# A head group's load in two parts, the second behind the next step's shift rows

## The reference

```python
x = x + _layernorm(attn(_layernorm(x)))
x = x + _layernorm(ffn(_layernorm(x)))
```

## Time and profile before

| | |
|---|---|
| median of three runs | 993.25 us |
| the profiled execution's own time | 992.39 us |
| its span, first to last instruction | 990.4 us |
| mean granted clock of PE | 0.999 |
| busy share of the span | PE 98%, DVE 72%, POOL 48%, ACT 39% |
| the hardware DMA queue | 144.49 MB, 47.4% of 16 engines' span |
| load of a group: queries, keys | 768 KB in 5.7 us, 192 KB in 6.1 us (medians from issue to landing) |

### The profile page before, as it was taken

The page is one execution under the profiler, slowest core; times in us unless marked ns, Lnnn a source line. Parts: engine busy times, 40 slices in busy tenths (PEclk is TensorE's granted clock), DMA queues, the critical chain, the costliest instruction groups (busy, mean ns, idle before and its releaser), DMA issues.

```text
span 990.4 us, 17190 instructions
## 1 busy us (share of the span) xinstructions
PE 973.8 (98%) x6315; PEld 801.0 (81%) x6315; DVE 716.3 (72%) x1968; ACT 382.4 (39%) x660; POOL 474.2 (48%) x478
## 2 busy tenths in 40 slices
PE   6999999999999999999999999999999999999997
PEld 6888898898886666666666679999999999999996
DVE  7778595775569999999999676666666666666655
ACT  6211120211138777787777662222222222222221
POOL 1455563644449999999998711111111111111110
PEclk9999999999999999999999999999999999999999
DMA  9764755467358777655555472332332332222201
GB/s 351 265 221 159 266 193 195 166 199 243 131 180 218 200 213 187 180 164 139 153 147 153 123 238 58 88 86 85 86 86 86 85 86 86 83 73 82 61 22 43
DMA packets 85411, 145.58 MB, mean 147 GB/s; under 512 B 7352, under 2 KB 46928, under 8 KB 82256
## 3 DMA queue, kind: packets, MB, share of 16 engines
q1 hardware_dynamic: 85328, 144.49, 47.4%
HBM read 93.07 MB, written 50.87 MB: 145 GB/s over the span
## 4 chain that ended last, share of the span: by engine, by line
PE 87%; DVE 7%; DMA 2%; issue 1%; POOL 1%; ACT 1%; POOLq 0%; SPq 0%; DVEq 0%
PE bank L1490 19%; PE bank L1492 19%; PE bank L1491 19%; PE bank L1595 8%; PE bank L1573 8%; PE bank L1611 7%; PE bank L1632 2%; PE bank L1638 1%; PE bank L1776 1%; DVE wq_l L1105 1%; DVE ln_st L1067 1%; DVE xt_l L1190 1%; DVE turn L1118 1%; DVE xt_raw L1182 1%; PE bank L1581 1%
## 5 line engine op out<-in xcount | busy, mean ns | idle before, releaser
L1141 DVE CUSTOM_DVE_ANT_0 bank<-bank,row_mask 128x384 f32<-128x384 f32 (+3 forms) x512 | 234.4, 518 | 35.9 <-PE bank L1573 35.7
L724 POOL TENSOR_TENSOR ln_rs<-ln_ve,minus_half 128x1 f32<-128x1 f32 x51 | 52.6, 1032 | 332.0 <-DVE ln_mm L1076 332.0
L940 ACT ACTIVATE prob<-bank 128x512 f32<-128x512 f32 x320 | 173.2, 599 | 24.5 <-PE bank L1595 15.7
L1492 PE MATMUL bank<-wf_l,xt_h 128*128 128x384 f32 (+3 forms) x384 | 130.1, 339 | 0.0
L1490 PE MATMUL bank<-wf_h,xt_h 128*128 128x384 f32 (+3 forms) x384 | 129.8, 338 | 0.2 <-DVE xt_l L1282 0.2
L1491 PE MATMUL bank<-wf_h,xt_l 128*128 128x384 f32 (+3 forms) x384 | 129.6, 338 | 0.0
L1490 PE MATMUL bank<-xt_h,wq_h 128*128 128x512 f32 x304 | 119.1, 392 | 0.9 <-DVE xt_l L1190 0.9
L1491 PE MATMUL bank<-xt_h,wq_l 128*128 128x512 f32 x304 | 118.5, 390 | 0.0
L1492 PE MATMUL bank<-xt_l,wq_h 128*128 128x512 f32 x304 | 118.4, 390 | 0.0
L1573 PE MATMUL bank<-k_t,q_t 96*128 96x384 f32 (+3 forms) x512 | 117.6, 327 | 0.0
L796 POOL TENSOR_TENSOR key_sum<-key_sum,prob 128x512 f32<-128x512 f32 x92 | 116.6, 1294 | 0.0
(11 more groups left out here) (131 smaller groups left out, 1931.8 us busy)
## 6 DMA issues: line engine op xcount, KB each, us to landing
q_t<-q_scratch SPq DMA_DIRECT2D x32, 768.0 KB, 5.7
q_scratch<-turn_h SPq DMA_DIRECT2D x32, 512.0 KB, 3.9
q_scratch<-turn SPq DMA_DIRECT2D x16, 512.0 KB, 4.7
att_scratch<-att SPq DMA_DIRECT2D x32, 256.0 KB, 3.0
at_raw<-att_scratch SPq DMA_DIRECT2D x16, 512.0 KB, 4.2
x<-x SPq DMA_DIRECT2D x16, 512.0 KB, 4.2
out<-z SPq DMA_DIRECT2D x15, 512.0 KB, 2.9
den_i<-inv_scratch SPq DMA_DIRECT2D x56, 128.0 KB, 5.0
```

What stands on the lines that cost most here:

```text
L724: nc.gpsimd.tensor_tensor(ln_rs[j][:], ln_ve[j][:], minus_half[:], ALU.pow).then_inc(count, 1)
L940: nc.scalar.activation(prob[n % 2][:, i, :, :].rearrange("p h q -> p (h q)"), score_bank(n, i)[:], ACT.Exp, scale=INV_SQRT_HD).then_inc(pr ...
L1141: last = nc.vector.tensor_tensor_reduce(out=row, in0=row, in1=row_mask[:, SEQ - w:SEQ], scale=1.0, scalar=LOWEST, op0=ALU.add, op1=ALU.max ...
L1492: return mm(dst, a_h, w_l, start=False, stop=stop, skip_group_check=True)
```

## The change

`load_group` gets an argument `parts`. Part 0 is the first half of the queries' columns (two heads), part 1 the other half and the keys. In SP's loop the call at the end of step n loads part 0 of group n + 4 only; part 1 of that group is issued in the next step, right behind that step's `load_shift`. A load has now three DMAs, so R0 waits for 48 counts per use of the slot instead of 32. The calls before the loop load both parts at once, as before.

```diff
-            def load_group(n):
+            def load_group(n, parts=(0, 1)):
...
-                sp.dma_start(q_dst[0:KROWS, :], q[:, cols]).then_inc(qk_loaded[s], 16)
-                sp.dma_start(k_dst[0:KROWS, :], k).then_inc(qk_loaded[s], 16)
+                half = REP * SEQ // 2
+                if 0 in parts:
+                    sp.dma_start(q_dst[0:KROWS, 0:half], q[:, cols][:, 0:half]).then_inc(qk_loaded[s], 16)
+                if 1 in parts:
+                    sp.dma_start(q_dst[0:KROWS, half:2 * half], q[:, cols][:, half:2 * half]).then_inc(qk_loaded[s], 16)
+                    sp.dma_start(k_dst[0:KROWS, :], k).then_inc(qk_loaded[s], 16)
...
             for n in range(NG):
                 if 0 < n < NG - 1:
                     load_shift(n + 1)
+                if n > 0 and n + SLOTS - 1 < NG:
+                    load_group(n + SLOTS - 1, (1,))
                 if 1 <= n < WO_LOADS:
                     load_out(n)
...
                 if n + SLOTS < NG:
-                    load_group(n + SLOTS)
+                    load_group(n + SLOTS, (0,))
...
                 if i == 0:
-                    pe.wait_ge(qk_loaded[s], 32 * (n // SLOTS + 1))
+                    pe.wait_ge(qk_loaded[s], 48 * (n // SLOTS + 1))
```

## The result

The changed kernel takes 1077.66 us (median of four runs, 1073.33 to 1083.87), the kernel before 993.3 (four runs beside them): a ratio of 1.0859, 95% interval 1.0837 to 1.0881. The direction and the wait at R0 were as forecast. The size was not: 84 us instead of 45, outside the range, because the wait is longer than estimated and because PE's clock falls, which the forecast had at 1 in 100.

The account below looks back on a forecast made before the run. PE bounds the kernel, busy 98% of the span. 28 steps x 1.69 us late at R0 = 47.3, less 2.4 of DMA waits, is +44.9 on 992.39; with 0.86 to the median, 1038 us, range 1008 to 1062.

Parts of the forecast that it names:

- the wait at R0: R0's weight load on PE waits for k_t or q_t some 1.7 us, 28 times, about 47 us.
- the sum: Whole kernel: 28 x 1.69 = 47.3 us of lateness less 2.4 is +44.9, giving 1038 us.
- The deadline: Part two, issued 2.17 us after T, has 2.85 us until R0's first weights; lateness comes back each step.
- the count of 28: Parts two are issued in SP's steps 1 to 28 (groups 4 to 31), each making R0 1.69 us late.
- I take 4.5: Part two's 576 KB land 4.5 us after the queries' issue (3.5 to 6.0), so R0 is 1.69 us late.
- the heavy rival: Instruction fetch beside part two adds 1.1 us in 19 steps, 21 us more, 1059 us; chance 0.12.
- I leave 1 in 100: PE's granted clock affected by R0's 1.7 us pause in each step; 1 in 100, inside the heavy case.
- I credit the change with all the waits for DMA: PE's waits for shift rows and keys in the heads' stage go: -2.4 us, bounds 0 and -2.4.
- Light: Rival: queue empty at part two's issue, landing 3.5 us, R0 late by 0.69, +17, 1010 us; chance 0.12.
- hidden: Rival: part two lands in time for R0 (2.8 us decides), only shift-row waits go, 991 us; chance 0.06.
- The estimate from the Trainium skill: Part two's landing by 2.0 us fixed plus bytes over 436 GB/s: 3.4 us, 0.55 late per step, some +13 us.

Follow-up runs that it names:

- experiment 1: Changed kernel with part two issued just ahead of load_shift(n+1) instead of behind it: 992.38 us, ratio to before 1.0001.
- experiment 5: Changed kernel, group cut by query position: keys and positions 0 to 255 first, 256 to 511 behind the shift rows, first read at R3: 992.61 us, ratio 1.0005.
- experiment 6: Changed kernel, SP waits behind part two's issue until that load has landed before issuing anything else: 1057.89 us, ratio 1.0656.
- Experiment 2: Changed kernel with extra matmuls on PE ahead of R0's wait for its load: six, 1064.95 us (ratio 1.0732); nine, 1061.66 us (1.07).
- experiment 4: Changed kernel with less in part two: first the keys alone (192 KB), 1005.01 us (1.013); then one head and keys (384 KB), 1041.03 us (1.0507).
- experiment 3: Changed kernel with R0 and R1 behind V3 instead of behind S0 in PE's order: 1053.02 us, ratio 1.0606.

## Why the prediction was wrong

The profiled execution lost 91.5 us where the sum had 44.9. Of the 46.6 us between them 17.8 are a longer landing of part two, 26.7 a lower clock, 0.6 a part of the credited 2.4 that did not come (1.8 of it came in these steps), and 1.5 lie outside the 28 steps.

- *The deadline* was right. T to part two's issue was put at 2.17 us and is 419.40 - 417.21 = 2.19. The loop shown is 3.64 from R0 to T (put at 3.77), 2.19, 4.75 to the landing and 0.04: 10.62 us. The lateness comes back each step, and the count of 28 holds. Experiments 1 and 5 show that it is the place against the use and nothing else of the change.
- *"I take 4.5"*, the landing of 576 KB from the queries' issue, was the term of the sum that was mis-sized. Measured by the issues and landings of the 28 steps it is 5.3 us on average: 4.9 in the 17 steps without a fetch beside the issue, 5.9 in the 11 with one. That makes 65.1 us of lateness (the 69.0 us of waits less 3.9) instead of 47.3. Of the 0.4 us in the 17 steps, 0.3 come from what SP issues right behind (experiment 6, steps without a fetch: 4.6 us). The wo_raw loads, from which the 4.5 came, are single DMAs; here the keys' issue follows 0.56 us behind the queries', not 0.35. The fetch's 1.0 us was in the heavy rival, with a price of 21 us for 19 steps; it came in 11. That it is the fetch is read from its packets' coincidence with an issue of over 1.2 us in all 11 steps and in none of the others; no run removed it, so that the fetch is the cause is not shown.
- *"I leave 1 in 100"* for the clock was the step that failed outright. The rows had no pause in this stage, so they could say nothing against it, and I read "unseen" as "unlikely". It cost 26.7 us of the profiled execution by the lengths of the steps. Experiment 2 shows that the pause brings it: with 39 us more of matmuls in the pauses, the low-clock steps cost 11.4 and then 4.7 us.
- *"I credit the change with all the waits for DMA"*, -2.4 us, was wrong in its reason. In the changed kernel's profile these waits are 0.5 us instead of 2.0, so most of the number came, but by luck. With 960 KB ahead of the shift rows (experiment 1) PE waits 2.1 us for them, with 768 KB (experiment 4, keys alone) not at all, with 576 KB (experiment 5) 1.9, and with the same 384 KB as in the change (experiment 6) 2.1. In the 28 steps of every profile here, all waits for shift rows are in steps with a fetch beside the shift rows. In the kernel before shift_l took 1.8 to 2.8 us without a fetch, the longer ones with the load ahead still in flight, and PE never waited. In the changed kernel it took 1.8 to 2.4 us in the 17 steps without a fetch at part two's issue and 2.9 to 3.7 in the 11 with one. So the load ahead does slow the shift rows a little, but each wait goes with a fetch. The rows had a hint of it: at 456.81 shift_l took 1.8 us, although the keys ahead, issued at 451.65, landed only 5.6 us later, at 457.2.
- The rivals: heavy (1059) was nearest and still low, since it had one of the two missing terms. Light and hidden fell: no part two landed under 4.3 us after its queries' issue. The estimate from the Trainium skill ("DMA: Bandwidth & Descriptors", section "Anatomy of one DMA — SWDGE (gpsimd) path"), 3.4 us, fell with them.

## What to carry to other kernels

Before moving a load later, write down where its first use stands in the consumer's order and how many microseconds of the consumer's own work lie between; a load that is late inside a loop is late in each turn. Cut a load by what is read last, not by what is even: halves by head were all due at the first unit, halves by position were free. Where the rows have no case of something, such as a pause of the bounding engine, they speak neither for nor against it: leave room in the range. And a pause in a PE-bound stage can cost more than its length: here 65 us of pauses brought 27 us of lower clock, while the 15 us of experiment 4's first kernel brought none in its profile.

## What the runs showed of the hardware that was not expected

- In the changed kernel and the two of experiment 2 the lower clock followed a pause of 1.59 to 3.5 us in 24 steps. The length of the pause alone does not decide: with one of 1.59 us the clock fell (nine matmuls), with one of 2.65 us in the changed kernel and one of 2.95 us in experiment 6 it did not.
- The clock can fall without a long pause: in experiment 3 PE's waits were under 0.8 us each, and every fourth or fifth step had a mean clock of 0.86 and was 1.55 us longer.
- In the changed kernel one 16 KB packet of the instruction queue beside part two's issue went with an issue of 1.28 to 1.87 us instead of 0.43 to 0.51 and a landing about 1 us later, in 11 of 11 steps. In experiment 6 eight packets fell on the keys' issue: that was slow too (1.15 to 1.59 us), but the keys landed no later.
